# Row numbers of 33 gathers copied at once, one span ahead, in a graph layer kernel on one core

## The reference, cut to what matters

```python
xn = _layernorm(x)
seg = edge_type * N_NODES + dst
h = xn
for l in range(3):                       # relu, relu, sigmoid
    agg = segment_sum(h[src], seg, num_segments=8 * N_NODES)
    h = act(einsum('rnd,rde->ne', agg.reshape(8, N_NODES, -1), W[l]) + h @ root[l] + bias[l])
x = x + h + linear_attention(xn)         # 4 heads of 32
x = x + mixture_of_experts(_layernorm(x))    # 8 experts, the best 2 for each node
```

## Time and profile before

| | us |
|---|---|
| median of 3 runs, without a profile | 3850.56 |
| span of the profiled execution | 4114.6 |
| POOL busy in it | 2472.2 (60%) |
| PE busy in it | 3088.8 (75%) |
| DVE busy in it | 1180.3 (29%) |
| ACT busy in it | 400.3 (10%) |
| mean granted TensorE clock | 0.795 |

### The profile page before, as it was taken

How to read it: one execution, slowest core, us unless ns; L and a number is a source line. 1 busy time by engine, 2 the same in 40 slices (tenths; PEclk the granted TensorE clock), 3 DMA queues, 4 the chain that set the end, 5 groups by cost and what they waited for, 6 DMA issues and landing times. The chain is left out here.

```text
span 4114.6 us, 51204 instructions
## 1 busy us (share of the span) xinstructions
PE 3088.8 (75%) x16304; PEld 2668.8 (65%) x16304; DVE 1180.3 (29%) x2874; ACT 400.3 (10%) x1010; POOL 2472.2 (60%) x2784
## 2 busy tenths in 40 slices
PE   3677677777787777878777777677877777877885
PEld 3566566666676666656666656566677767766775
DVE  4222222222223322222122222333333333333323
ACT  1000000000000000000000000001112112211232
POOL 5666666666666666666666656665555555555233
PEclk8778787777778777677777677878888888898898
DMA  6333333433344333333333333334455455455675
GB/s 167 116 114 117 114 119 114 126 116 114 117 118 130 92 90 93 92 94 90 92 93 92 92 105 91 90 92 135 150 164 162 151 158 172 148 161 162 205 249 200
DMA packets 276975, 524.33 MB, mean 127 GB/s; under 512 B 60783, under 2 KB 180331, under 8 KB 276716
## 3 DMA queue, kind: packets, MB, share of 16 engines
q0 software_dynamic: 121152, 331.40, 27.6%
q1 hardware_dynamic: 154396, 190.17, 14.6%
q10 hardware_dynamic: 1296, 1.24, 0.1%
HBM read 458.71 MB, written 63.91 MB: 127 GB/s over the span
## 5 line engine op out<-in xcount | busy, mean ns | idle before, releaser
L703 POOL DMA_INDIRECT arena<-rows_dram,arena x2396 | 2275.6, 950 | 1157.0 <-issue 705.7
L1888 PE MATMUL bank<-arena 128*128 128x128 f32 x4836 | 1084.4, 335 | 485.5 <-DMA arena<-rows_dram,arena 240.8
L1888 PEld LDWEIGHTS bank<-arena 128*128 128x128 f32 x4836 | 888.0, 232 | 665.5 <-issue 330.2
L1487 DVE TENSOR_TENSOR arena<-arena,bank 128x256 f32 x807 | 338.2, 419 | 2433.4 <-remote 1401.9
L1892 PE MATMUL bank<-arena 128*128 128x128 f32 x4836 | 901.9, 324 | 152.1 <-issue 145.4
L1892 PEld LDWEIGHTS bank<-arena 128*128 128x128 f32 x4836 | 792.0, 235 | 185.7 <-issue 184.5
L1748 PE MATMUL bank<-arena 128*128 128x256 f32 x2400 | 657.3, 411 | 95.5 <-issue 52.2
L1748 PEld LDWEIGHTS bank<-arena 128*128 128x128 f32 x2400 | 466.6, 208 | 177.8 <-issue 125.6
L1406 DVE TENSOR_TENSOR arena<-bank,arena 128x1408 f32<-128x1408 f32 x222 | 355.3, 1603 | 11.6 <-issue 11.6
L1802 PE MATMUL bank<-arena 128*128 128x128 f32 x1152 | 172.8, 307 | 68.1 <-DVE arena L1335 38.3
L1802 PEld LDWEIGHTS bank<-arena 128*128 128x128 f32 x1152 | 162.0, 220 | 76.0 <-issue 74.9
(11 more groups left out here) (227 smaller groups left out, 1533.1 us busy)
## 6 DMA issues: line engine op xcount, KB each, us to landing
arena<-in_L_ffn_W_dram SPq DMA_DIRECT2D x112, 512.0 KB
arena<-in_L_ffn_W_dram SPq DMA_DIRECT2D x44, 1024.0 KB
arena<-rows_dram,arena POOLq DMA_INDIRECT x2418
xs_dram<-zslot SPq DMA_DIRECT2D x25, 1224.0 KB
arena<-xs_dram SPq DMA_DIRECT2D x56, 136.0 KB
rows_dram<-arena SPq DMA_DIRECT2D x50, 128.0 KB
arena<-in_L_gnn_weights_dram SPq DMA_DIRECT2D x6, 1024.0 KB
arena<-ys_dram SPq DMA_DIRECT2D x8, 640.0 KB, 8.1
```

Of the source, the lines that this page charges most:

```text
L703: nc.gpsimd.indirect_dma_start(out=gath[:, slot, :], out_offset=None, in_=rows_dram[l], in_offset=bass.IndirectOffsetOnAxis(ap=idx_ring[:, ...
L1487: nc.vector.tensor_tensor(acc, acc, edge_sum(l, q).rearrange("p (k r n) -> p k r n", k=KD, r=REL), ALU.add).then_inc(S["tile_add"], 1)
L1888: nc.tensor.matmul(edge_sum(l, q)[:, 0:WC], gath[:, slot, 0:P], onehot[:, slot, :], start=first, stop=last)
```

## The change

`idx_ring` gets 66 columns, two halves of 33. In place of a copy of 11 columns ahead of each chunk, GpSimd copies the 33 columns of the next span into the other half once in a span, behind the `group_mm` wait of chunk 1, and doesn't wait for it there; the first chunk of the next span waits for a count of these copies (`ring_made`). At the end of the first two layers the copy for the next layer's first span is in two parts (11 and 22 columns). ScalarE fills what GpSimd doesn't copy at the start: 22 columns as before and the other 44 in one copy. The bounds of the `group_mm` waits are the same; they, and the waits at the layer's start, are now `wait_apart`. VectorE's wait in the last span is for the last of the new copies, which is issued a span earlier.

```diff
+RINGS = NSPAN + 1
-        idx_ring = carve(SLOTS_G).bitcast(I32)
+        idx_ring = carve(2 * SLOTS_G).bitcast(I32)
+        def ring_half(l, par):
+            h = (par + l) % 2
+            return idx_ring[:, SPAN * h:SPAN * (h + 1)]
+        def rings(l, s):
+            return 1 if l == 0 and is_first(s) else RINGS * l + s.m
-                def gather(slot):
+                def gather(slot, at):
-                        in_offset=bass.IndirectOffsetOnAxis(ap=idx_ring[:, slot:slot + 1], axis=0)).then_inc(s_gath[slot], 16)
+                        in_offset=bass.IndirectOffsetOnAxis(ap=at[:, slot:slot + 1], axis=0)).then_inc(s_gath[slot], 16)
-                    def ring(s, a, n):
-                        used = -(-CH * (a + 1) // GT)
+                    def freed(s, a):
                         if is_first(s):
-                            freed = GROUPS * (l - 1) + (SG * (NSPAN - 1) - (-CH // GT) if a == 0 else GROUPS) if l > 0 else 0
-                        else:
-                            freed = GROUPS * l + SG * (s.m - 1) + (CH * (a + 2)) // GT
-                        wait(pool, "group_mm", freed)
-                        if l > 0 and is_first(s) and a == CPS - 1:
-                            wait(pool, "miss_mm", l)
-                        part = idx_part if l > 0 and is_first(s) and a == 0 else idx_i[:, bass.ds(CH * (CPS * s.m + a), n)]
-                        nc.gpsimd.tensor_copy(idx_ring[:, CH * a:CH * a + n], part).then_inc(S["ix_ready"], 1)
+                            return GROUPS * (l - 1) + (SG * (NSPAN - 1) - (-CH // GT) if a == 0 else GROUPS) if l > 0 else 0
+                        return GROUPS * l + SG * (s.m - 1) + (CH * (a + 2)) // GT
+                    def next_rows(s):
+                        o = ring_half(l, 1 - s.par)
+                        if not is_last(s):
+                            if l > 0 or not is_first(s):
+                                nc.gpsimd.tensor_copy(o, idx_i[:, bass.ds(SPAN * (s.m + 1), SPAN)]).then_inc(S["ring_made"], 1)
+                        elif not final:
+                            nc.gpsimd.tensor_copy(o[:, 0:CH], idx_part).then_inc(S["ring_made"], 1)
+                            nc.gpsimd.tensor_copy(o[:, CH:SPAN], idx_i[:, CH:SPAN]).then_inc(S["ring_made"], 1)
                     def span(s):
+                        at = ring_half(l, s.par)
                         for a, n in chunks_of(s):
                             if l == 0 and is_first(s) and a < AHEAD:
                                 continue
-                            ring(s, a, n)
+                            wait_apart(pool, "group_mm", freed(s, a))
+                            if a == 1:
+                                next_rows(s)
                             if l > 0 and is_first(s) and a == 1:
-                                wait(pool, "last_st", 16 * l)
-                            wait(pool, "ix_ready", CHUNKS * l + CPS * s.m + a + 1)
-                            pool.nop(nofuse=True)
+                                wait_apart(pool, "last_st", 16 * l)
+                            if l > 0 and is_first(s) and a == CPS - 1:
+                                wait_apart(pool, "miss_mm", l)
+                            if a == 0 or l == 0 and is_first(s):
+                                wait_apart(pool, "ring_made", rings(l, s))
                             for j in range(n):
-                                gather(CH * a + j)
+                                gather(CH * a + j, at)
             for a in range(AHEAD):
                 nc.scalar.copy(idx_ring[:, CH * a:CH * (a + 1)], idx_i[:, CH * a:CH * (a + 1)]).then_inc(S["ix_ready"], 1)
+            nc.scalar.copy(idx_ring[:, CH * AHEAD:2 * SPAN], idx_i[:, CH * AHEAD:2 * SPAN]).then_inc(S["ring_made"], 1)
-                                    dve.wait_ge(S["ix_ready"], CHUNKS * LAYERS)
+                                    dve.wait_ge(S["ring_made"], RINGS * LAYERS - 2)
```

More of the change, by code:

```diff
@@ L328, in gps_layer @@
         names = """src_in edge_in wrel_in mixw_in ffw_in win_moved out_st
-            const pads ids first_st agg_clean src_made edges_made edge_turned edge_back viol_sum flag_set
+            const pads ids first_st src_made edges_made edge_turned edge_back viol_sum flag_set
             var_made sd_made nm_made xn_made xa_made
-            ix_ready hot_ready tile_mm group_mm tile_add folded node_ready stage_full agg_zero node_mm hn_made
+            ix_ready ring_made hot_ready tile_mm group_mm tile_add folded node_ready stage_full agg_zero node_mm hn_made
             rows_st last_st miss_mm miss_out hn_turned hT_made
@@ L687, in _ @@
                                     pattern=[[-1, P]], channel_multiplier=1).then_inc(S["const"], 1)
-            nc.gpsimd.memset(agg_w, 0.0).then_inc(S["agg_clean"], 1)
+            nc.gpsimd.memset(agg_w, 0.0).then_inc(S["const"], 1)
             pool.wait_ge(S["src_in"], 3 * 16)
@@ L764, in chunk @@
                         for j in range(n):
-                            gather(CH * h + j)
+                            gather(CH * h + j, idx_ring)
                     def general(t, p0):
@@ L966, in _ @@
             act.wait_ge(S["first_st"], 16 * (NG + LAYERS - 1))
-            act.wait_ge(S["agg_clean"], 1)
+            act.wait_ge(S["const"], 10)
             for l in range(LAYERS):
@@ L1391, in _ @@
             dve.wait_ge(S["flag_set"], 1)
-            dve.wait_ge(S["agg_clean"], 1)
+            dve.wait_ge(S["const"], 10)
             dve.wait_ge(S["win_moved"], 32)
```

## The result

The changed kernel took 3724.68 us (median of 4 runs, 3717.56 to 3731.16) against 3852.57 for the kernel before on the same chip (4 runs): a ratio of 0.9671, 95% interval 0.9655 to 0.9687, or 127.9 us less. The forecast was 3737, range 3706 to 3810, faster with a chance of 0.86.

A forecast was written before the change was run, and what follows sets the result against it. POOL's queue was taken to pace a plain run nearly throughout. Gains of 86.3 us (first two layers), 16.5 (third layer) and 10.7 (experts' stage) summed to 113.5, so 3850.6 - 113.5 = 3737 us, range 3706 to 3810.

The forecast's parts named there:

- POOL paces a plain run: Whole kernel: POOL's queue alone sums to 3768 us of the plain 3850.6, leaving some 83 us for waits.
- The border, 0.67 us x 220 = 147.4: Between chunks on POOL: without the copy ahead, the gap falls from 0.97 to 0.30 us, saving 147.4 us.
- the three parts of the sum (144, 27 and 48): Chunk borders counted: 144 in the first two layers, 27 in the third, three in each of 16 experts' spans.
- The copy, 0.20 us x 75 = 15.0: On POOL, once a span: 75 added copies of 33 columns at 0.20 us each cost 15.0 us.
- The experts' stage, 10.7 us: Its 16 spans, where POOL waits for PE: only 16 x 0.67 = 10.7 us gained in place of 29.0.
- The price behind an unmet wait: Where PE holds chunk 0: release to first gather shrinks from 0.94 to some 0.30 us, about 0.67 gained.
- The first rival: PE holds chunk 0 of all 73 spans in plain runs too: only 49 us gained, 3802 us; chance 0.24.
- The third rival: Landings set the pace; the rest for the fourth gather's landing grows by what was saved: 3851 us; chance 0.08.
- PE holds every span: Holes in PE are in plain runs too; all 73 spans gain only 0.67 us: 49 us, 3802; chance 0.24.
- the nop drains the queue: At chunk borders the apart wait's nop makes the gap 1.25 us, not 0.97: 77 us slower, 3927; chance 0.06.
- nothing moves: Landings are the pace and the rest at the fourth gather's landing takes back the gain: 3851 us; chance 0.08.
- the guess behind it: Holes in PE's rows behind bursts of node matmuls were a cost of recording, gone in a plain run.

The follow-up runs named there:

- e1: The kernel before, unchanged, profiled a second time: 3857.22 us, span 3855.1.
- e7: The kernel before, with only the rest loosened: after a chunk's fifth gather it waits for the second's landing, not the fourth's; 3581.90 us.
- e3: The changed kernel, but the 33 columns are copied at the span's own first chunk and waited for there: 3782.76 us.
- e4: The changed kernel with a wait for the copy's completion right behind it at chunk 1: 3760.84 us.
- e6: The changed kernel, but after a chunk's fifth gather it waits for the landing of the second, not of the fourth: 3449.80 us, ratio 0.8945.
- e5: The changed kernel with each chunk's group_mm wait and nop issued five times in place of once: 3726.63 us.
- e9: The changed kernel, but after a chunk's fifth gather it waits for the landing of the first, not of the fourth: 3427.64 us, ratio 0.8877.

## Why the prediction was right, point by point

*POOL paces a plain run.* Right, and more so than I dared. The sum over POOL's queue left 83 us for its waits in a plain run; in e1 a wait for PE shows at one border only (1.2 us). Reading it from a disturbed profile was possible only because the sum was set against the plain time.

*The border, 0.67 us x 220 = 147.4.* Measured 0.97 to 0.30 where nothing but the copy stands there, as forecast, though the three parts of the sum (144, 27 and 48) count 219 of the 220 borders. The total, 147.7 us between e1 and the changed kernel with the new copies in it, holds something else too: in e1 POOL stops for some 2 us longer at three borders, with nothing to wait for in any view, and at the same three in e7. One of them:

```profile
418.53 0.97 POOL L703 DMA_INDIRECT arena<-rows_dram,arena  x1 [2.75 <-issue]
```

The changed kernel has none of these three (e3 and e4 have one each). They are 6 us of the 147.7, they don't belong to the wait for the copy, and why they are gone isn't shown.

*The copy, 0.20 us x 75 = 15.0.* Too dear. The copy itself takes 0.22 us, but a gather needs 0.30 us of lead in any case, and the copy lies inside it: the border grows by 0.09, some 6.5 us over 75. "I take the 0.30 of two gathers" for the gap behind the copy was the step that failed; it is 0.16. The Trainium skill's price for an element of a copy (GPSIMD Engine Reference, section 3.1), 1.8 to 2.6 cycles at 1.2 GHz, makes an estimate of 0.03 to 0.05 us for the 22 further columns. The trace has 0.222 against 0.198 us, so 0.024, or 1.3 cycles: a little under it.

*The experts' stage, 10.7 us.* The worst of the terms. I let TensorE hold 16 spans there, since the disturbed profile showed 111.3 us of it. In e1 the stage takes 852.0 us (2728.1 to 3580.1), not 975, and its copies wait for nobody; the changed kernel needs 823.8 (2626.7 to 3450.4), 28.2 less, close to the full gain of 29.0 that I had set aside. Borders gave 34.0 of it, rests took 8.2 back.

*The price behind an unmet wait.* Even with TensorE holding the spans, 10.7 would have been too much. I let the way from release to gather shrink from 0.94 to 0.30. The same border, the first of the second layer's second span, is held by PE in both kernels with the looser rest, e7 and e6. In e7 the group's last matmuls end at 1154.49:

```profile
1153.66 0.83 PE L1892 MATMUL bank<-arena 128*128 128x128 f32 x6
1154.72 0.19 POOL L734 COPY arena<-arena 128x11 int32 x1 [5.53 <-PE bank L1892]
1155.68 0.97 POOL L703 DMA_INDIRECT arena<-rows_dram,arena  x1 [0.78 <-POOL arena L734]
```

and in e6 at 1122.85:

```profile
1122.02 0.83 PE L1913 MATMUL bank<-arena 128*128 128x128 f32 x6
1123.77 0.94 POOL L715 DMA_INDIRECT arena<-rows_dram,arena  x1 [6.70 <-PE bank L1913]
```

That is 1.19 us from the matmuls' end to the gather against 0.92, a gain of 0.27 and not 0.67. The first rival, priced at 0.67 x 73 = 49 us by the same step, was too dear likewise; 0.27 x 73 makes some 20 us, as an estimate. By the Trainium skill (Perfetto Trace Analysis, per-engine timelines), on which I had hung a gain near 0, the gather behind an unmet wait has still to be decoded and pushed. The trace agrees in so far as the gather starts 0.92 us behind the end of the wait, not 0.30; a gain of 0 it is not.

*Missing altogether:* the longer rests, 28.4 us. The row I leaned on, a DMA share of 0.33 to 0.39, is a mean; 1.2 MB in one burst isn't seen in it. The third rival named longer rests, but as the pace of the landings and with all of the gain; it was a fifth, and in the first layer it came from the stores' bursts.

So 113.5 were forecast, and the plain runs gave 127.9, the two profiled spans 131.0. In the spans: 6.7 us too little for the 59 copies outside the experts' stage, 17.5 too little for that stage, and 20.2 too much for leaving out the other rests (28.4 - 8.2). That makes 117.5. The rest are things I hadn't expected to move, outside the experts' stage: 5.0 us in the gathers' own time (a gather right behind a copy takes 0.97 us and not 0.95, and 145 copies fewer make some 3 of it), 3.3 in the gaps between all other gathers, 4 in two of the three pauses, and about 1 behind the last gather. That the forecast came within 15 us is in part luck, since an error of 24.2 on one side met one of 20.2 on the other.

*The rivals.* "PE holds every span" fell by e1 and e4, "the nop drains the queue" by e5 and by 0.30 at every border, "nothing moves" by the result. The forecast for the profiled execution itself (4045 to 4065) was wrong, with the guess behind it: the next profile read 3724.

## What to carry to other kernels

Here an engine that copies its next operands in its own queue and waits for that copy pays the whole round trip at each step, 0.97 us, though the copy is 0.2; copied one step ahead into a second buffer, the satisfied wait isn't seen and the copy costs 0.09 us. Set the sum of the suspected queue against the plain time before believing the waits of one profile; where they differ by 7%, as here, profile once more, and look for an engine that stands idle with nothing to wait for. And when one engine's steps move against another's, look where bursts on other queues now fall.

## What the runs showed that I had not expected

Loosening one wait, on which no data depends, is worth twice the change studied: from 3724.7 to 3427.6 us in e9, and 277 us in the kernel before (3858.8 to 3581.9 in e7). A landing comes 2.7 us behind the issue in the median, so some 1.8 us behind the end of the descriptors (0.95 us). The fifth gather's descriptors are done 1.25 us behind the fourth's, so a wait for the fourth's landing has some 0.55 us still to go, and behind the landing another 0.76 us pass before the next gather starts: together the 1.3 us of a usual rest. In e1 and in the changed kernel none of the 217 rests was met in time (the shortest idle was 1.16 us); with the wait for the gather three places back 177 of 217 were in e6 (0.30 us, as between any two gathers), and with one more place 200 of 217 in e9.

Five satisfied waits with nops in a row cost nothing that shows behind a gather, and a copy behind one costs 0.09 us.
